# Chunk 0's x added by accumulating loads instead of PE transposes, its second layer norm one stage later, with four smaller moves, in an eight-core layer kernel

## The reference, cut to what matters

```python
h    = rmsnorm(layernorm(x)) * gamma                 # x: (8, 2048, 1024) f32
q, kv, a = split(h @ w_qkva.T); a = sigmoid(a)
y[t] = a[t] * y[t-1] + kv[t]                         # scan over the sequence
x    = x + q * y
g    = layernorm(x)
gate = softmax(g @ Wg + bg)                          # 8 experts, hidden size 128
out  = x + sum_e gate[e] * (relu(g @ W1[e] + b1[e]) @ W2[e] + b2[e])
```

## Time and profile before

| | |
|---|---|
| median of 3 runs | 329.07 us (328.75 to 329.85) |
| the profiled execution, its own time | 326.83 us |
| its span, slowest core (5) | 325.3 us |
| spans of the cores | 322.1 us (0, 4) to 325.3 us (3, 5) |
| granted TensorE clock | 0.999 to 1.000 on every core |
| busy: PE, DVE, ACT, POOL | 312.9, 187.7, 96.4, 59.1 us |
| stages on core 5, start of the first matmul | A0 19.6, A1 69.9, F0 115.9, A2 145.4, F1 189.0, A3 218.4, F2 262.0, F3 292.7 us |

### The profile page before, as it was taken

One profiled execution on the slowest core, in us unless ns is written; L12 is line 12 of the kernel. 1 busy time (PEld: TensorE's weight loads), 2 busy tenths in 40 slices (PEclk: granted clock), 3 DMA queues, 4 the chain that ended last, 5 costly groups with the idle time before them and its releaser, 6 DMA issues.

```text
span 325.3 us, 4956 instructions; the slowest of 8 cores (322.1 to 325.3 us)
## 1 busy us (share of the span) xinstructions
PE 312.9 (96%) x1605; PEld 141.3 (43%) x1605; DVE 187.7 (58%) x417; ACT 96.4 (30%) x150; POOL 59.1 (18%) x120
## 2 busy tenths in 40 slices
PE   7589998999999999999999999999999999999996
PEld 3245443454444444444444444444444444444442
DVE  1835389354778993362778683362778346634333
ACT  1572424663336315004225504004225520200000
POOL 4870004301311222001131322001131310000000
PEclk9999999999999999999999999999999999999999
DMA  6999999999981301875900301977000300173033
GB/s 137 207 152 174 236 216 189 240 173 257 175 198 21 133 0 36 159 226 185 295 7 0 133 0 34 163 221 232 2 0 1 132 0 0 54 192 147 0 128 130
DMA packets 18377, 40.53 MB, mean 125 GB/s; under 512 B 9680, under 2 KB 9840, under 8 KB 17328
## 3 DMA queue, kind: packets, MB, share of 16 engines
q1 hardware_dynamic: 15056, 25.47, 27.1%
q0 software_dynamic: 3296, 14.75, 24.3%
HBM read 40.25 MB, written 8.42 MB: 150 GB/s over the span
## 4 chain that ended last, share of the span: by engine, by line
PE 77%; DMA 15%; DVE 3%; POOL 2%; issue 1%; SPq 0%; DVEq 0%; POOLq 0%
PE ps L641 38%; PE ps L710 17%; PE ps L728 17%; DMA wq<-wqd 12%; DMA xtok<-xt 2%; PE ps L703 2%; PE ps L404 1%; DVE sc L654 1%; POOL wq L534 1%; POOL w L230 1%; PE ps L309 1%; POOL wq L531 1%; PE ps L418 1%; DVE h1g L616 0%; DVE bst L265 0%
## 5 line engine op out<-in xcount | busy, mean ns | idle before, releaser
L641 PE MATMUL ps<-pb,wq 128*128 128x512 bf16 x768 | 170.6, 379 | 2.4 <-DMA wq<-wqd 1.4
L641 PEld LDWEIGHTS ps<-pb,wq 128*128 128x128 bf16 x768 | 74.3, 98 | 90.6 <-issue 6.3
L677 POOL TENSOR_TENSOR xb<-xb,sc 128x512 f32<-128x512 f32 x24 | 30.4, 1268 | 156.6 <-DVE sc L663 117.2
L710 PE MATMUL ps<-pb,w 128*128 128x512 bf16 x256 | 57.0, 379 | 0.0
L728 PE MATMUL ps<-h1g,w 128*128 128x512 bf16 x256 | 56.8, 379 | 0.0
L648 ACT ACTIVATE asig<-ps 128x512 f32<-128x512 f32 x32 | 19.1, 597 | 110.3 <-PE ps L641 97.9
L654 DVE TENSOR_TENSOR_SCAN sc<-asig,carry,ps 128x512 f32<-128x512 f32 x24 | 30.7, 1278 | 30.8 <-ACT sqr L392 19.8
L731 DVE TENSOR_TENSOR xb<-ps,xb 128x512 f32<-128x512 f32 x32 | 22.1, 692 | 30.1 <-PE ps L728 30.1
L710 PEld LDWEIGHTS ps<-pb,w 128*128 128x128 bf16 x256 | 24.3, 98 | 30.1 <-issue 2.2
L728 PEld LDWEIGHTS ps<-h1g,w 128*128 128x128 bf16 x256 | 24.4, 98 | 29.9 <-issue 1.8
L713 DVE SCALAR_TENSOR_TENSOR h1g<-ps,grep 128x512 bf16<-128x512 f32 x32 | 22.1, 692 | 26.3 <-PE ps L710 26.1
(11 more groups left out here) (113 smaller groups left out, 169.5 us busy)
## 6 DMA issues: line engine op xcount, KB each, us to landing
xtok<-xt SPq DMA_DIRECT2D x12, 512.0 KB, 10.1
outd<-xb SPq DMA_DIRECT2D x12, 512.0 KB, 3.8
wq<-wqd POOLq DMA_DIRECT2D x7, 768.0 KB, 26.8
grep<-gscr SPq DMA_DIRECT2D x4, 1024.0 KB, 5.3
xb<-xd SPq DMA_DIRECT2D x8, 512.0 KB, 5.5
w<-xt POOLq DMA_DIRECT2D x4, 512.0 KB, 31.7
xb<-xd POOLq DMA_DIRECT2D x4, 512.0 KB, 50.3
w<-w1d POOLq DMA_DIRECT2D x2, 1024.0 KB, 55.8
```

The costliest lines, as they stand in the source:

```text
L641: mm[i] = PE.do(lambda e, k=k: e.matmul(ps[banks[i]][:], wq[:, j, i, k, :], hbc[:, k, :], start=(k == 0), stop=(k == KC - 1)), h[k] if j = ...
L677: x2 = POOL.do(lambda e: e.tensor_tensor(xc[:, j, :], xc[:, j, :], sc[s][:], ALU.add), at, x_t[c][j])
L710: t = PE.do(lambda e, k=k: e.matmul(ps[b][:], w1[:, e_, k, :], xbf_of[c][:, k, :], start=False, stop=(k == KC - 1)), C[c]["xbf"][k] if e_ ...
```

## The change

- Chunk 0 no longer turns x on PE. The q multiply writes the product straight into `xb`, and four loads on POOL's queue (`add_xd`) add x to it as they land, two feature blocks each. PE's 32 transposes and DVE's 8 adds go; 2 MB more are loaded.
- LN2 of chunk 0 moves: its `cs_step`s from A0 to groups 0 to 2 of A1, its 16 row matmuls into one step at (3, 0), `ln2_small` to (3, 1) to (5, 0). The squares lie in `xn` instead of `sqr`.
- POOL's queue is ordered anew: the two later x loads of chunk 1, W1 and b2 come after the adds, at the end of A0. The token loads of chunk 2 wait for chunk 1's first new x instead of chunk 0's last transpose.
- LN1 of chunk 1 takes its second pair of token blocks on DVE (`ln1_small_dve`). LN1 of chunk 2 is done in two pairs, and its statistics move from A1 to experts 0 to 3 of F0.
- `back` turns the gates of chunks 0 to 2 by a transposing DMA from SP; chunk 3's stays on PE (`back_pe`).
- Weights of groups 5, 6 and 7 are loaded in thirds, one for each projection, each with its own semaphore.
- The very last output tile is done in two halves of 256 tokens, each stored by itself.

```diff
+        def add_xd(q):
+            t = POOL.dma(lambda e: e.dma_start(out=xb[0][:, 2 * q:2 * q + 2, :], in_=xd[0, :, q * 1024:(q + 1) * 1024],
+                                               accum_op=ALU.add), chan(f"d_xa{q}"), C[0]["at"][2 * q + 1])
+            C[0]["x2"][2 * q] = t
+            C[0]["x2"][2 * q + 1] = t
...
+            for i in range(lo, hi):
+                C[c].setdefault("r1t", {})[i] = C[c]["r1"]
+        def ln1_small_dve(c, lo, hi):
+            t = C[c]["seed"]
+            for it in range(3):
+                out = r1 if it == 2 else ry
+                t = DVE.do(lambda e: e.tensor_tensor(ya[:, sl], ry[:, sl], ry[:, sl], ALU.mult), t)
+                t = DVE.do(lambda e: e.scalar_tensor_tensor(ya[:, sl], ya[:, sl], -0.5, va[:, sl], ALU.mult, ALU.mult), t)
+                t = DVE.do(lambda e, out=out: e.scalar_tensor_tensor(out[:, sl], ya[:, sl], 1.5, ry[:, sl], ALU.add,
+                                                                     ALU.mult), t,
+                           C[c - 1]["xn"][NT - 1] if it == 2 else None)
+            C[c]["r1"] = DVE.do(lambda e: e.scalar_tensor_tensor(nb1[:, sl], mv[:, sl, 0], -1.0, r1[:, sl],
+                                                                 ALU.mult, ALU.mult), t)
...
-                                   C[c]["r1"], xn_free[i])
+                                   C[c]["r1t"][i] if c else C[c]["r1"], xn_free[i])
...
         def cs_step(c, k):
-            b = sq_i["i"] % NSQ
-            sq_i["i"] += 1
             prior = {0: None, 1: C[0].get("pe_q"), 2: C[0].get("pe_h1"), 3: C[1].get("pe_h1")}[c]
             src = xb[c % 2][:, k, :]
+            if c == 0:
+                b, sq, free = None, xn[:, k // 2, (k % 2) * TC:(k % 2 + 1) * TC], xn_free[k // 2]
+            else:
+                b = sq_i["i"] % NSQ
+                sq_i["i"] += 1
+                sq, free = sqr[b][:], sq_free[b]
             t1 = ACT.do(lambda e: e.activation(xbf_of[c][:, k, :], src, AF.Copy), C[c]["x2"][k], prior)
-            t2 = ACT.do(lambda e: e.activation(sqr[b][:], src, AF.Square), C[c]["x2"][k], sq_free[b])
+            t2 = ACT.do(lambda e: e.activation(sq, src, AF.Square), C[c]["x2"][k], free)
             C[c]["xbf"][k] = t1
...
+        def rows_step(c, k, n_tiles=4):
-            for kk in range(k - 3, k + 1):
+            for kk in range(k - n_tiles + 1, k + 1):
...
-                        tok, psR_free[bank] if k == 3 else None, wg_t, ms["sele"])
+                        tok, psR_free[bank] if kk < 4 else None, wg_t, ms["sele"])
                     n += 1
-                sq_free[b] = t
+                if c == 0:
+                    xn_free[kk // 2] = t
+                else:
+                    sq_free[b] = t
...
         def back(c):
+            gb = gro[c % 2]
+            if c < NCH - 1:
+                ta = SP.dma(lambda e: e.dma_start(out=gb[:].rearrange("p (i t) -> p i t", t=128),
+                                                  in_=tm[:].rearrange("p i m -> p (i m)"), transpose=True),
+                            back_ch, st["sm"], *gro_free[c % 2])
+                st["tm"] = ta
+            else:
+                ta = back_pe(c)
+            C[c]["gro"] = ta
+            go = SP.dma(lambda e: e.dma_start(out=gscr[c], in_=gb[E:2 * E, :]), bounce_ch["go"], ta)
+            C[c]["gi"] = SP.dma(lambda e: e.dma_start(out=grep[:], in_=gscr[c].partition_broadcast(128)),
+                                bounce_ch["gi"], go, st["grep"])
+            gro_free[c % 2] = [go]
...
         def load_wq(j):
-            if j == 0:
+            if j == 0 or j > 4:
                 wq_t[j] = [POOL.dma(lambda e, i=i: e.dma_start(
-                    out=wq[:, 0, i], in_=wqd[0, :, i * 1024:(i + 1) * 1024]), chan(f"d_wq0{i}")) for i in range(3)]
+                    out=wq[:, j, i], in_=wqd[j, :, i * 1024:(i + 1) * 1024]), chan(f"d_wq{j}{i}")) for i in range(3)]
             else:
                 wq_t[j] = [POOL.dma(lambda e: e.dma_start(out=wq[:, j], in_=wqd[j]), chan(f"d_wq{j}"))] * 3
...
-        load_w1(0)
-        load_xd(1, 2, lane=POOL)
-        load_w1(1)
-        load_xd(1, 3, lane=POOL)
+        b2_t = []
+        def load_b2():
+            for r in range(4):
+                t = POOL.dma(lambda e, r=r: e.dma_start(out=b2p[32 * r:32 * r + E, :], in_=b2d), b2_ch, ms["b2"])
+            b2_t.append(t)
...
                 proj(2)
-                at = DVE.do(lambda e: e.tensor_tensor(sc[s][:], ps[bq][:], sc[s][:], ALU.mult), mm[2], cy)
+                dst = xc[:, j, :] if c == 0 else sc[s][:]
+                at = DVE.do(lambda e: e.tensor_tensor(dst, ps[bq][:], sc[s][:], ALU.mult), mm[2], cy)
                 ring_free[bq] = at
                 if c == 0:
-                    bx = ring_take()
-                    for i in range(NT):
-                        tx = PE.do(lambda e, i=i: e.matmul(
-                            ps[bx][:, i * 128:(i + 1) * 128], xtok[:, i, j * 128:(j + 1) * 128], ident[:],
-                            start=True, stop=True, is_transpose=True),
-                            xt_t[0][i], id_t, ring_free[bx] if i == 0 else None, tick=(i == NT - 1))
-                    x2 = DVE.do(lambda e: e.tensor_tensor(xc[:, j, :], ps[bx][:], sc[s][:], ALU.add), tx, at)
-                    ring_free[bx] = x2
-                    C[0]["tx"] = tx
+                    sc_free[s] = at
+                    C[0].setdefault("at", []).append(at)
                 else:
                     x2 = POOL.do(lambda e: e.tensor_tensor(xc[:, j, :], xc[:, j, :], sc[s][:], ALU.add),
                                  at, x_t[c][j])
-                sc_free[s] = x2
-                C[c]["x2"][j] = x2
+                    sc_free[s] = x2
+                    C[c]["x2"][j] = x2
                 if j == KC - 1:
                     C[c]["pe_q"] = mm[2]
                 hook((j, 2))
...
+        def last_tile(b):
+            c, d = NCH - 1, KC - 1
+            xc, gb = xb[c % 2], gro[c % 2]
+            half = TC // 2
+            toks = []
+            for hf in range(2):
+                sl = slice(hf * half, (hf + 1) * half)
+                pb_ = ps[b] if hf == 0 else psR[0]
+                for e_ in range(E):
+                    t = PE.do(lambda e, e_=e_, sl=sl, pb_=pb_: e.matmul(
+                        pb_[:, sl], w2[:, d, e_, :], h1g[:, e_, sl], start=False, stop=(e_ == E - 1)),
+                        C[c]["h1g"][e_], w2_t[d // 4], tick=(e_ == E - 1))
+                o = DVE.do(lambda e, sl=sl, pb_=pb_: e.tensor_tensor(xc[:, d, sl], pb_[:, sl], xc[:, d, sl], ALU.add), t,
+                           C[c]["cs"][d][1], C[c]["cs"][d][2])
+                C[c]["st"][d + hf] = SP.dma(lambda e, hf=hf, sl=sl: e.dma_start(
+                    out=outd[c, :, d * TC + hf * half:d * TC + (hf + 1) * half], in_=xc[:, d, sl]),
+                    chan(f"d_stl{hf}"), o)
...
+                if c == NCH - 1 and w is b2w and n == 4:
+                    PE.do(lambda e: e.matmul(psR[0][:], w(7)[96:128, :], gb[96:128, :], start=True, stop=False),
+                          psR_free[0], tick=False)
...
-                banks = open_quad(lambda n: b2p[:, n * 128:(n + 1) * 128], q, b2_t)
+                banks = open_quad(b2w, q, b2_t[0])
                 for i in range(4):
-                    outtile(q + i, banks[i])
+                    if c == NCH - 1 and q + i == KC - 1:
+                        last_tile(banks[i])
+                    else:
+                        outtile(q + i, banks[i])
...
-        stat_hooks(hk, 0)
         gate = {}
         for lo, p in ((0, ((4, 0), (4, 1), (5, 1))), (2, ((5, 0), (5, 1), (6, 1)))):
-            add(hk, p[0], lambda lo=lo: (ln1_bn(1, lo), ln1_bn(1, lo + 1)))
-            add(hk, p[1], lambda lo=lo: (ln1_seed(1, lo, lo + 2), ln1_small(1, lo, lo + 2)))
+            add(hk, p[0], lambda lo=lo: ln1_bn(1, lo))
+            add(hk, p[0] if lo == 0 else p[1], lambda lo=lo: ln1_bn(1, lo + 1))
+            add(hk, p[1], lambda lo=lo: (ln1_seed(1, lo, lo + 2), (ln1_small_dve if lo else ln1_small)(1, lo, lo + 2)))
             add(hk, p[2], lambda lo=lo: (ln1_norm(1, lo), ln1_norm(1, lo + 1)))
         add(hk, (5, 0), lambda: gate.update(t=gate_sums()))
+        add(hk, (6, 2), lambda: (add_xd(0), add_xd(1), add_xd(2)))
         phase_a(0, hk)
         wgs_tok = gate["t"]
+        add_xd(3)
+        load_xd(1, 2, lane=POOL)
+        load_xd(1, 3, lane=POOL)
+        load_w1(0)
+        load_w1(1)
+        load_b2()
         load_w2()
-        for i in range(NT):
-            load_xt(2, i, C[0]["tx"])
-        def bn_hooks(hooks, c):
-            for n, p in enumerate([(5, 2), (6, 2), (7, 1), (7, 2)]):
+        def bn_hooks(hooks, c, places):
+            for n, p in enumerate(places):
                 add(hooks, p, lambda n=n: ln1_bn(c, n))
         hk = {}
-        ln2_hooks(hk, 0, A_PLACES)
         stat_hooks(hk, 1)
+        for k, p in enumerate([(0, 2), (0, 2), (1, 1), (1, 1), (1, 2), (2, 1), (2, 1), (2, 2)]):
```

(37 more changed lines are left out.)

20 lines of the change are left out of this document (10 added, 10 removed).

## The result

The changed kernel takes 330.83 us in the median of 13 runs (329.51 to 333.53), the kernel before 329.07 in as many. The ratio is 1.0058, with a 95% interval of 1.0032 to 1.0085: slower by 0.6%, where 0.9% faster was forecast, and just outside the range.

What follows compares the result with a forecast made beforehand. PE was taken as the bound, busy 312.9 of 325.3 us. The terms -3.9 + 1.0 + 0.5 - 0.44 - 0.1 gave -2.9 us, so 329.07 became 326.2 us, range 323.9 to 330.5.

Steps and rivals of the forecast that it cites:

- the gates' sum: Chunk 0's gates before F0: transpose, write and spread load end at 114.8, 4 us over quiet; PE waits 0.5 us.
- Rival 3: Gates late for F0: the three transfers end near 119, DVE and PE wait 4.7 us, 330.4 us; chance 0.10.
- The doubled case: Chunk 0's gates: each of the three transfers doubles beside W2's load, ending at 121.
- A0: Transposes out, thirds in: group 6 starts at 53.0 and ends 4.1 us earlier; A1 starts at 65.4, 4.5 us earlier.
- The adds: Four accumulating x loads on POOL's queue: 2.6 us each, against 1.6 plain; W1 lands at 96.1, no wait.
- Rivals 1 and 2: Late load queue: adds of 4.0 us, 331.2 us, chance 0.14; adds of 3.2 us, W1 at 98.5, 328.5 us, chance 0.13.
- The price of 3.2: POOL's queue: by the skill's half-rate rule an add costs 3.2 us instead of 1.6, W1 lands at 98.5.
- LN2 late for `w1_parts`: End of A1: chunk 0's later LN2 delays group 4's scan and multiply; PE waits 0.3 + 0.4 us for two banks.
- The gain of 0.5 in A1: PE's 0.5 us wait at F0's opening goes, since chunk 2's statistics leave the DVE's list in A1.
- a term of 1.0 in the text: F0's second opening: PE waits 1.0 us for the DVE, which has chunk 2's statistics between the experts.
- Rival 5: A0: the thirds land together and don't help, 3.6 us less gained there, 328.6 us; chance 0.07.
- rival 4: A1 and F0: the new waits don't come, LN2 and statistics fit, the queue is in time, 324.3 us; chance 0.16.

Runs made afterwards that it cites:

- e2: Changed kernel with W2 loaded only after chunk 0's transposed gates have landed: 324.94 us, ratio 0.9927 to the kernel before.
- e9: Changed kernel with one more load, half of W2's bytes, queued behind W2 into an unread DRAM buffer: 336.69 us, ratio 1.0301 to the kernel before.
- e4: Changed kernel with W2 in eight loads of 4 KB rows instead of two of 16 KB rows: 329.71 us, ratio 1.0067 to the kernel before.
- e10: Changed kernel with only W2's second half held back until chunk 0's gates are turned: 329.66 us, ratio 1.0085 to the kernel before.
- e5: e1's kernel with chunk 0's gates written out five times in a row, so `grep` comes late: 332.75 us, ratio 1.0155 to the kernel before.
- e8: e1's kernel with the weights of groups 5 to 7 each whole in one load again: 328.56 us, ratio 1.0029 to the kernel before.
- e6: e1's kernel with chunk 2's statistics back in A1 instead of F0: 325.49 us, ratio 0.9939 to the kernel before.
- e1: Changed kernel with the gates of all chunks turned on PE again: 325.47 us, ratio 0.994 to the kernel before.
- e11: e2's kernel again in more rounds, on another chip: 323.40 us, ratio 0.9893 to the kernel before.

## Why the prediction was wrong, and where it was right

**The step that failed** is the gates' sum: "Each of the three transfers can double ... nearer to the quiet rows I take 4 us more." In place of 2.5 + 1.4 + 5.0 us, which the quiet transfers take, the first took 11.3 alone, to the end of W2, and the others their quiet time. The end came at 119.2, not 114.8. Rival 3 had this case to the letter ("ends near 119, wait 4.7, 330.4", measured 119.2, 4.7 on the DVE and 4.1 on PE, 330.83), at a chance of 0.10. That chance was wrong, and my own numbers should have told me: W2 until about 109, the transpose from 100. (The doubled case was also mis-added: 100.1 + 2 x 10.8 is 121.7, not 121.)

I asked by what factor a transfer beside a busy queue is slowed; the question was how many packets it has, since each waits for one of the other queue. The trace of before has no transposing DMA beside a load on POOL's queue, but it has both numbers: its transposing DMAs go in packets of 256 bytes, and W2's packets take 0.62 us. The gates are 128 KB, so 512 packets, 32 for each of 16 engines, and 32 turns of 0.62 us are 20 us (an estimate), far more than the 9 that W2 had left by the forecast: by these numbers the transpose would end with W2.

e2, e9, e4 and e10 show the mechanism: queue empty, 2.5 us; its end 6.2 us later on core 1, 17.7; the other queue's packets a quarter as long, 92 packets in a microsecond instead of 20, and on five cores an end before W2's; the queue's end moved forward, 4.7. The write has 16 packets and was slowed by less. What stays open is why the first packet moves 2.9 to 4.2 us after the issue on the cores of the changed kernel, against 1.1 to 1.3 in an empty queue; it is not the rest of SP's own queue alone, since that was through within 1 us of the issue on core 0 of e4. The Trainium skill (DMA: Bandwidth & Descriptors, "Queues, rings and completion order") says that a DMA engine takes turns between its queues packet by packet. The traces of e4 and e9 agree: 362 packets and 368, 100 and 101.

**The step that was missing:** I priced a wait by its own length and put what the clock takes behind it at nothing. In the changed kernel, the waits of 2.05 us (core 7) to 4.40 us (core 6) at F0's second opening were followed by 32 matmuls in 8.2 to 9.4 us, those of 0.9 us (cores 4 and 5) by 32 in 7.08. e5 shows that the clock falls without a transposing DMA, behind the wait alone. With these two the sum closes on core 3: 323.9 forecast for the profiled execution, + 1.4 for A1's start at 66.83 instead of 65.4, + 2.6 for a wait of 4.1 instead of 1.0 + 0.5, + 2.2 of clock is 330.1; it took 329.81. Its median lies 1.0 us above that, where I had taken the 2.2 of the kernel before; so rival 3's 330.4 came out near the 330.83 with a term missing and one too many.

**A0.** Forecast: group 6 from 53.0 behind a short wait, A1 from 65.4. Core 3 has 54.35, a wait of 2.0 and 66.83; core 5 has a wait of 0.3 and 63.6. Right in kind, between these two cores in size. Core 4 fared worse: a wait of 3.0 us ahead of group 6, and the clock fell behind it, so that 39 matmuls took 10.48 us where core 3 has 40 in 8.84. PE's row and the window:

```profile
55.42 10.48 PE L685 MATMUL ps<-pb,wq 128*128 128x512 bf16 x39 [3.02 <-DVE carry L703]
...
52.00:60.00 8.00, 4.98 (x16) 1.82 (x15) 6.32 (x22) 2.97 (x3) 2.67 (x7) 0.79 1.08 190
```

Its `grep` came late too, at 118.5, but so did its F0, at 116.4, so that it waited there no longer than core 5. The thirds are worth 2.9 us (e8); the prediction took 4.1 for them and the transposes.

**The adds.** 2.6 us each forecast, 2.5 measured (2.7 for the last on core 3); W1 at 96.1 forecast, 95.7 measured, and no wait for it. Rivals 1 and 2 fell. The plain load is cheaper than I had it, 1.2 to 1.3 us, so an add is close to twice a plain load. That agrees with the rule of the Trainium skill cited in the prediction (Collectives: The Full Stack, "Why ReduceScatter is half of AllGather"). The price of 3.2 that I worked out from it was off only because my 1.6 for the plain load was.

**A1.** LN2 late for `w1_parts`: 0.3 + 0.4 forecast, 0.6 + 0.4 measured. LN2's last instruction 100.1 forecast, 101.0 measured.

**F0.** The wait at the second opening is 0.9 us wherever `grep` is in time (1.0 forecast). The gain of 0.5 in A1 for it stood against a term of 1.0 in the text; with the statistics back in A1 (e6) the waits there are 0.9 + 0.7, and the time is the same.

**The sum.** With the gates repaired in either way, the kernel is where the forecast's other terms put it: -2.9 us forecast; e1 -2.0 (0.994), e2 -2.4 (0.9927), e11 -3.5 (0.9893). Rival 5 fell with e8, and rival 4 with the waits of 0.6, 0.4 and 0.9 us, which all came.

## What to carry to other kernels

Before a small transfer is put on the critical path beside a long queue, count its packets, not its bytes: with turns one for one, each costs a packet of the other queue, and a transposing DMA has many (512 for 128 KB here). If that comes to more than the queue has left, the transfer ends with the queue. The remedy was not to undo the edit but to issue the bulk load behind the small transfer (0.7% and 1.1% faster than before on two chips instead of 0.6% slower); by time alone it can't be told from e1, which undid the edit (0.6% faster); half of it was no remedy, since the next small transfer then met the other half. Price a wait of PE of this length at what it lasts plus what the granted clock takes behind it, here 1.1 to 2.3 us more, and look at the clock by core before anything else.
